# Two-layer graph network: one picked tile fewer per iteration in each layer

## Chip, cores and metric

The kernel runs on one core of a Trainium2 chip. The metric is the device time of one execution in microseconds (us); a lower time is better. The kernel before took 6166.7 us (median of 3 runs, 6165.09 to 6170.27).

## The reference

A graph has 12500 nodes of 32 features and 400000 edges, each with a source node `src` and a destination node `dst`, sorted by `dst`. Two layers run one after the other, each on the layer-normed and rectified features.

```
h = relu(layernorm(x))
# layer 0: a small network per edge, mean over the edges of a destination
m   = relu(concat(h[src], edge_attr_16) @ w1a + b1a) @ w1b + b1b
agg = segment_sum(m, dst) / max(count, 1)
x   = x + relu(concat(h, agg) @ w2a + b2a) @ w2b + b2b
h = relu(layernorm(x))
# layer 1: a sum per destination
x   = x + (1 + eps) * h + segment_sum(relu(h[src] + edge_attr_32), dst)
```

The costly step is `h[src]`: for each of the 400000 edges one row has to be fetched by an index.

## The kernel before, in words

**Tiles, chunks, iterations.** 128 edges make a tile, five tiles a chunk (slot k = 0 to 4), five chunks an iteration. There are 125 iterations of 25 tiles in each layer. All of it is written out by hand, with counting semaphores between the engines; a `Turn` is an iteration, written as half and offset so that two iterations stand in one loop body, and `sum_near_windows(layer, scope)` holds the loops of both layers.

**Two ways to fetch rows.** A tile's 128 source rows come in one of two ways. *Gathered*: GpSimd (POOL) issues an indirect DMA that reads them from DRAM (`gathers`, the issue is recorded at L953), from `projected_rows` (the source part already multiplied by w1a) in layer 0 and `hidden_rows` in layer 1. *Picked*: all nodes lie in SBUF as `part_high` and `part_low`, node = 100 * partition + block, in 7 pieces of 14 blocks (the last of 16). For each piece TensorE multiplies the pieces by a 0/1 matrix `owner_hot`, which selects a partition for each edge (`sum_pieces`, L977): 14 matmuls per picked tile. VectorE then selects the block within the piece with one multiply and one reduction (`select`, L1218 and L1229). In layer 0 the picked rows are transposed on TensorE (`turn_pick`, L991), copied by ScalarE into the lower 32 rows of the chunk's edge block (`copy_pick`, L1091), and enter the chunk's edge product (`edge_products`, L998) as further rows of the contraction, so that bank columns of that tile hold the whole sum. In layer 1 they are written where a gather would have put them.

`PICK_TABLE` lists the picked tiles: slot, tile, row in the owner list, place. Seven exist: tile 4 of each slot, tile 3 of slots 1 and 3. Layer 0 uses the five of tile 4, so 20 tiles per iteration are gathered; layer 1 uses all seven and gathers 18. `tiles_in(k, parity)` is how many tiles of chunk k are gathered, `picks_of(k, turn)` which picks it has.

**Hot rows.** ScalarE makes `owner_hot` for the next iteration in three batches, slots 0 and 1, 2 and 3, and 4 (`make_hots`): seven squares per batch (L1080) and one relu over the batch (L1085). Their size goes with the number of picks in the batch.

**The order within a step.** Each engine runs through k = 0 to 4. TensorE in step k: `sum_pieces` for slot k + 3 (layer 1: k + 2), in layer 0 the edge product of slot k + 1 and the transpose of slot k + 2, then `scatter` of chunk k - 1, a one-hot product that sums messages by destination into a window of 48 nodes (L1007). VectorE: add of the edge part to the gathered rows (`add_edges`, L1251), in layer 1 the split in two parts (L1258, L1262), window add (L1273), one-hot of the destinations (L1233), then `select`. ScalarE: relu (`rectify`, L1103 and L1105 in layer 0, L1098 in layer 1), edge load at k = 0, `copy_pick`, `make_hots`.

**What holds the gathers.** Before the gathers of chunk k POOL waits until the chunk's buffer has been rectified in the iteration before (`rectified`), and for pacing until picks further ahead have been summed (`pieces_summed`) and, halfway through the chunk, until half of the next pick is (`halves_summed`); `picks_ahead` says which. The gathers of the first iteration have no pacing wait. One semaphore per slot counts landed gathers, and `add_edges` waits for it.

**Between the layers** stand the mean, the node network of layer 0, the second layer norm and the split, which the change does not touch, and after each loop a check for edges outside the windows. Its semaphore counts are worked out from `LAYER_PICKS[0]`.

Of the kernel before, what the change touches and what calls it, by code (L numbers as in the profile page):

```python
# [6 lines left out]
P = 128  # L7
# [4 lines left out]
TILES = 5  # L12
CHUNK = TILES * P
SLOTS = 5
# [13 lines left out]
ACT = mybir.ActivationFunctionType  # L28
# [6 lines left out]
PICK_TABLE = (Pick(0, 4, 1, 0), Pick(1, 4, 2, 1), Pick(1, 3, 0, 5), Pick(2, 4, 3, 2), Pick(3, 4, 4, 3),  # L35
              Pick(3, 3, 5, 6), Pick(4, 4, 6, 4))
PICK_ROWS = len(PICK_TABLE)

LAYER_PICKS = ((tuple(pick for pick in PICK_TABLE if pick.tile == TILES - 1),) * 2,
               (PICK_TABLE, PICK_TABLE))  # L40

BATCH_SLOTS = ((0, 1), (2, 3), (4,))
BATCH_OF_SLOT = (0, 0, 1, 1, 2)
# [5 lines left out]
def number(turn):  # L49
    return 2 * turn.half + turn.offset  # L50


def odd(turn):
    return turn.offset % 2
# [6 lines left out]
def before(turn, even_count, odd_count):  # L61

    passed = even_count * ((turn.offset + 1) // 2) + odd_count * (turn.offset // 2)
    return (even_count + odd_count) * turn.half + passed
# [9 lines left out]
def since(homes, n):  # L74


    count = len(homes)
    for back in range(1, count + 1):
        if homes[(n - back) % count] == homes[n]:
            return back  # L80


def gnn_kernel(nc, x, src_cols, src_picks, dst_cols, dst_rows, edge16, edge32, w1a, b1a, w1b_t, b1b,
# [4 lines left out]
    PICK_ROW = P - D  # L88
    CHUNKS = edge16.shape[0]
    H1 = b1a.shape[0]  # L90
# [45 lines left out]
    with ExitStack() as ctx:  # L136
# [3 lines left out]
        def sem(name):  # L140
            return ctx.enter_context(nc.semaphore(name))
# [58 lines left out]
        def edge_t(k, parity):  # L200
            return edges[:, parity * SLOTS + k, 0:P]
        gathered = [sb(f"gathered{k}", [P, TILES, H1]) for k in range(SLOTS)]
        messages = sb("messages", [P, SLOTS * TILES, SUMS])
        message = [messages[:, k * TILES:(k + 1) * TILES, :] for k in range(SLOTS)]
# [4 lines left out]
        bank = [ctx.enter_context(nc.psum_tensor(f"bank{k}", [P, PSUM_COLS], F32)) for k in range(8)]  # L209
# [126 lines left out]
        def piece_of(part, j):  # L336

            b = piece_blocks(j)
            return part[0:NP, b.start * D:b.stop * D].rearrange("p (f b) -> p f b", f=D)
# [47 lines left out]
        def gathered_rows(k, row):  # L387

            flat = gathered[k][:, :, :].rearrange("p t n -> p (t n)")[:, 0:TILES * row]
            return flat.rearrange("p (t n) -> p t n", n=row)  # L390
# [14 lines left out]
        def prepare(scope):  # L405
# [58 lines left out]
            with nc.Block() as block:  # L464
# [165 lines left out]
                def _(dve):  # L630
# [48 lines left out]
                    nc.vector.memset(ln_eps[:, :], LN_EPS).then_inc(ln_eps_ready, 1)  # L679
                    nc.vector.memset(zero_col[:, :], 0.0)  # L680
                    nc.vector.memset(edges[64:PICK_ROW, :, 0:P], 1.0)
                    dve.wait_ge(counted, 2)
                    nc.vector.tensor_copy(window_f[:, :], window_i[:, :])
                    nc.vector.tensor_scalar(minus_piece[:, :], piece_i[:, :], -1.0, None, ALU.mult)
# [37 lines left out]
        def sum_near_windows(layer, scope):  # L722
# [3 lines left out]
            width, row, table = (SUMS, H1, projected_rows) if layer == 0 else (2 * D, D, hidden_rows)  # L726
# [9 lines left out]
            summed = sem(f"summed{layer}")  # L736
            picks = LAYER_PICKS[layer]
            PICKS = [len(some) for some in picks]
            ROUND = sum(PICKS)
# [8 lines left out]
            picks_copied = sem("picks_copied") if layer == 0 else None  # L748
# [60 lines left out]
            def pick_hot(pick, j, parity):  # L809

                b = BATCH_OF_SLOT[pick.slot]
                hots = batch_hot(b, parity).rearrange("p (j s e) -> p j s e", j=PIECES, e=P)
                return hots[:, j, pick.row - rows_of_batch(picks[parity], b).start, :]

            if layer == 0:
                LOOK, SELECT = 3, 3
                edge_home = [k % 3 for k in range(SLOTS)]
                pick_home = [5 + n % 2 for n in range(ROUND)]
                wide_home = [0, 1, 2, 0, 1] * 2
            else:  # L820
                LOOK, SELECT = 2, 1
                pick_home = [0, 1, 2, 5, 6, 7, 0, 1, 2, 5, 6, 7, 2, 5]
            window_banks = (3, 4)

            summands = width if layer == 0 else SUMMANDS
# [17 lines left out]
            def picks_of(k, turn):  # L843
                return [n for n, pick in enumerate(picks[odd(turn)]) if pick.slot == k]

            def tiles_in(k, parity):
                return TILES - sum(pick.slot == k for pick in picks[parity])

            def picks_before(turn):
                return before(turn, *PICKS)  # L850

            def chunks_before(turn):
                return before(turn, SLOTS, SLOTS)

            def place_in_round(n, turn):
                return n + (PICKS[0] if odd(turn) else 0)
# [22 lines left out]
            with nc.Block(no_gpsimd_drain=True) as block:  # L879
# [87 lines left out]
                def _(pe):  # L967
                    def sum_pieces(n, turn, early=False):

                        pick, home = picks[odd(turn)][n], place_in_round(n, turn)  # L970
                        if n == picks_of(BATCH_SLOTS[BATCH_OF_SLOT[pick.slot]][0], turn)[0]:
                            pe.wait_ge(owners_hot[BATCH_OF_SLOT[pick.slot]], number(turn) + 1)
                        if early or layer and since(pick_home, home) < 6:
                            pe.wait_ge(pieces_placed, picks_before(turn) + (n + ROUND + 1 - since(pick_home, home)))
                        for m, (j, part) in enumerate(products_of_a_pick):
                            rows = piece_of(part, j)
                            last = nc.tensor.matmul(  # L977
                                bank[pick_home[home]][:, 0:PITCH * D].rearrange(
                                    "p (f b) -> p f b", b=PITCH)[:, :, 0:rows.shape[2]],
                                pick_hot(pick, j, odd(turn)), rows,  # L980
                                start=(m == 0), stop=(m == len(products_of_a_pick) - 1))
                            if m == len(products_of_a_pick) // 2 - 1:
                                last.then_inc(halves_summed, 1)
                        last.then_inc(pieces_summed, 1)
# [9 lines left out]
                    def edge_products(k, turn):  # L994
                        if k == 0:
                            pe.wait_ge(edge_in, 16 * number(turn) + 16)
                        pe.wait_ge(picks_copied, picks_before(turn) + (picks_of(k, turn)[0] + ROUND + 1))
                        nc.tensor.matmul(bank[edge_home[k]][:, 0:TILES * H1], edge_t(k, odd(turn)),  # L998
                                         w_edge[:, :, :].rearrange("p t n -> p (t n)"),
                                         start=True, stop=True).then_inc(multiplied, 1)  # L1000
# [37 lines left out]
                    for k in range(LOOK):  # L1038
                        for n in picks_of(k, FIRST):
                            sum_pieces(n, FIRST, early=layer == 0 and n >= 2)  # L1040
# [26 lines left out]
                def _(act):  # L1067
# [26 lines left out]
                    def rectify(k, turn):  # L1094

                        if layer:
                            act.wait_ge(rows_split, chunks_before(turn) + (k + 1))
                            nc.scalar.activation(message_parts[:, k, :, 0:2 * D], message[k][:, :, 0:2 * D],  # L1098
                                                 ACT.Relu).then_inc(rectified, 1)
                        else:  # L1100
                            act.wait_ge(added, chunks_before(turn) + (k + SLOTS + 1))
                            tiles = tiles_in(k, odd(turn))
                            nc.scalar.activation(message[k][:, TILES - 1, 0:row],  # L1103
                                                 bank[edge_home[k]][:, (TILES - 1) * H1:TILES * H1], ACT.Relu)
                            nc.scalar.activation(message[k][:, 0:tiles, 0:row], gathered_rows(k, row)[:, 0:tiles, :],  # L1105
                                                 ACT.Relu).then_inc(rectified, 1)

# [257 lines left out]
        def sum_far_windows(layer):  # L1365
# [6 lines left out]
            gather_in = gathers_in[0]  # L1372
            near = [TILES - sum(pick.slot == k for pick in LAYER_PICKS[0][0]) for k in range(SLOTS)]
            gathers_done = [16 * ITERS * (near[k] + TILES * layer) for k in range(SLOTS)]
# [331 lines left out]
        with ExitStack() as own:  # L1706
            self_part = sb("self_part", [P, BLOCKS, H2], scope=own)
            with ExitStack() as scope:
                prepare(scope)
            with ExitStack() as scope:  # L1710
                sum_near_windows(0, scope)
                sum_far_windows(0)
            with ExitStack() as scope:
                update_nodes(scope)
        with ExitStack() as scope:
            sum_far_windows(1)
            sum_near_windows(1, scope)
# [32 lines left out]
```

## Time and profile before

| | |
|---|---|
| median of 3 runs | 6166.7 us |
| profiled execution, its own time | 6167.25 us |
| its span, first to last instruction | 6165.2 us |
| granted TensorE clock, mean | 0.991 |
| layer 0, first to last gather | 63 to 3199 us |
| layer 1, first to last gather | 3291 to 6134 us |
| busy, PE / VectorE / ScalarE / GpSimd | 5919.7 / 3754.2 / 4351.2 / 4544.9 us |

Times are microseconds unless marked ns. PE is the matmul side of TensorE, PEld its weight loads, DVE VectorE, ACT ScalarE, POOL GpSimd. A matmul's shown duration overlaps the next one's, so the pace of PE is read from start times. For POOL, busy is the issue of an indirect DMA; what stands in brackets is idle time just before and what ended it. "issue" there means that the profile shows nothing that it waited for.

### The profile page before, as it was taken

The page shows a single profiled execution, that of the slowest core. Times are in us where ns is not written, and L with a number is a line of the kernel's source. Part 1 is how long each engine was busy: PE and PEld are TensorE (multiplying, and loading weights), DVE is VectorE, ACT ScalarE, POOL GpSimd, SP SyncE. Part 2 cuts the span into 40 slices and gives each one's busy share as a digit, 9 for nine tenths or more (in the row PEclk, how much of TensorE's full clock was granted, in tenths as well). Part 3 has the DMA queues.
Part 4 walks back from the last instruction along what each step waited for, and adds up shares of the span by engine and source line. Part 5 has one row for each costly group of instructions (what it writes and reads, how often), then busy time and mean ns, then how long its engine had stood idle before and what let it go on. Part 6 is the DMA issues. An engine that isn't in the chain of part 4 may idle for free. (4 is left out here: it accounts for less than half of the span.)

```text
span 6165.2 us, 106642 instructions
## 1 busy us (share of the span) xinstructions
PE 5919.7 (96%) x32834; PEld 5085.6 (82%) x32835; DVE 3754.2 (61%) x9052; ACT 4351.2 (71%) x8692; POOL 4544.9 (74%) x4799
## 2 busy tenths in 40 slices
PE   7999999999999999999988999999999999999999
PEld 5887777777777777777777888888888888888888
DVE  6554444444444444444447777777777777777776
ACT  5766666666666666666656777777777777777775
POOL 5777777777777777777755777777777777777776
PEclk9999999999999999999998999999999999999999
DMA  4222222222222222222221222222221222222221
GB/s 116 66 69 65 65 65 67 66 67 65 65 65 68 65 66 65 65 65 68 65 50 45 52 52 51 49 53 53 52 51 48 53 52 52 50 50 52 53 53 41
DMA packets 331462, 367.43 MB, mean 60 GB/s; under 512 B 87161, under 2 KB 256536, under 8 KB 331166
## 3 DMA queue, kind: packets, MB, share of 16 engines
q0 software_dynamic: 152000, 160.05, 13.8%
q1 hardware_dynamic: 46276, 130.67, 6.5%
q10 hardware_dynamic: 133146, 76.25, 4.4%
q8 instruction: 17, 0.28, 0.0%
q14 instruction: 23, 0.19, 0.0%
HBM read 358.17 MB, written 8.46 MB: 59 GB/s over the span
## 5 line engine op out<-in xcount | busy, mean ns | idle before, releaser
L977 PE MATMUL bank<-part_high,owner_hot 125*128 125x448 f32 (+1 forms) x10500 | 4011.6, 382 | 181.3 <-ACT owner_hot L1085 147.9
L977 PE MATMUL bank<-part_low,owner_hot 125*128 125x448 f32 (+1 forms) x10500 | 3897.7, 371 | 0.0
L953 POOL DMA_INDIRECT gathered<-projected_rows,indices x2500 | 2368.5, 947 | 779.2 <-issue 692.6
L953 POOL DMA_INDIRECT gathered<-hidden_rows,indices x2250 | 2151.7, 956 | 693.7 <-issue 576.0
L977 PEld LDWEIGHTS bank<-part_high,owner_hot 125*128 125x128 f32 x10500 | 1980.7, 189 | 414.1 <-ACT owner_hot L1085 162.3
L977 PEld LDWEIGHTS bank<-part_low,owner_hot 125*128 125x128 f32 x10500 | 1979.4, 189 | 197.7 <-issue 0.2
L1080 ACT ACTIVATE owner_hot<-owner_in,minus_piece 125x256 fp32r<-125x256 f32 (+2 forms) x3948 | 1591.6, 484 | 37.9 <-PE bank L977 11.6
L1085 ACT ACTIVATE owner_hot<-owner_hot 125x1792 fp32r<-125x1792 f32 (+1 forms) x750 | 1276.0, 1701 | 23.8
L1218 DVE SCALAR_TENSOR_TENSOR hidden<-window_f,places_now,bank 128x512 f32<-128x512 f32 x1500 | 1101.7, 734 | 121.8 <-PE bank L977 121.4
L1251 DVE TENSOR_TENSOR gathered<-gathered,bank 128x384 f32<-128x384 f32 x625 | 346.0, 554 | 1323.6 <-DMA gathered<-projected_rows,indices 1257.2
L1103 ACT ACTIVATE messages<-bank 128x96 f32<-128x96 f32 x625 | 157.5, 252 | 923.4 <-DVE gathered L1251 917.0
L1098 ACT ACTIVATE message_parts<-messages 128x320 fp32r<-128x320 f32 x625 | 292.6, 468 | 640.1 <-DVE messages L1262 640.1
L1007 PEld LDWEIGHTS bank<-hidden,messages 128*97 128x97 f32 x6250 | 601.8, 166 | 168.7 <-issue 160.0
L1007 PE MATMUL bank<-hidden,messages 128*97 128x48 f32 x6250 | 613.9, 245 | 5.0 <-ACT messages L1105 5.0
L1229 DVE TENSOR_REDUCE gathered<-hidden 128x32 f32<-128x512 f32 x875 | 600.2, 686 | 30.2
L998 PE MATMUL bank<-w_edge,edges 128*128 128x480 f32 x1250 | 607.3, 567 | 4.4 <-ACT edges L1091 4.4
L1080 ACT ACTIVATE owner_hot<-hidden,minus_piece 125x384 fp32r<-125x384 f32 x1302 | 585.6, 531 | 19.3 <-issue 14.6
L1251 DVE TENSOR_TENSOR gathered<-gathered,edges 128x160 f32<-128x160 f32 x625 | 205.7, 329 | 489.0 <-DMA gathered<-hidden_rows,indices 470.2
L1229 DVE TENSOR_REDUCE wide_rows<-hidden 128x32 f32<-128x512 f32 x625 | 428.8, 686 | 21.5
L1007 PEld LDWEIGHTS bank<-onehot_r,message_parts 128*66 128x66 f32 x3125 | 277.3, 139 | 84.1 <-ACT message_parts L1098 35.0
L1105 ACT ACTIVATE messages<-gathered 128x384 f32<-128x384 f32 x625 | 323.4, 517 | 0.0
L1007 PE MATMUL bank<-onehot_r,message_parts 128*66 128x48 f32 x3125 | 270.4, 213 | 15.3 <-ACT message_parts L1098 14.2
(125 smaller groups left out, 2478.1 us busy)
## 6 DMA issues: line engine op xcount, KB each, us to landing
owner_in<-owner_rows SPq DMA_DIRECT2D x188, 448.0 KB
edges<-in_edge ACTq DMA_DIRECT2D x124, 400.0 KB
gathered<-projected_rows,indices POOLq DMA_INDIRECT x2500
gathered<-hidden_rows,indices POOLq DMA_INDIRECT x2250, 2.4
hidden<-owner_rows SPq DMA_DIRECT2D x62, 448.0 KB
edges<-in_edge ACTq DMA_DIRECT2D x124, 200.0 KB
projected_rows<-projected SPq DMA_DIRECT2D x25, 168.0 KB
sources<-in_src_cols SPq DMA_DIRECT2D x1, 1562.5 KB, 6.8
```

Source lines behind the costliest of these rows:

```text
L953: pool.indirect_dma_start(gathered_rows(k, row)[:, t, :], None, table, bass.IndirectOffsetOnAxis(ap=index(k, odd(turn))[:, t:t + 1], axis= ...
L977: last = nc.tensor.matmul(bank[pick_home[home]][:, 0:PITCH * D].rearrange("p (f b) -> p f b", b=PITCH)[:, :, 0:rows.shape[2]], pick_hot(pi ...
L998: nc.tensor.matmul(bank[edge_home[k]][:, 0:TILES * H1], edge_t(k, odd(turn)), w_edge[:, :, :].rearrange("p t n -> p (t n)"), start=True, s ...
L1007: last = nc.tensor.matmul(bank[window_home(k, turn)][0:summands, 0:WINDOW], summand(k, t), onehot[k][:, t, :], start=(t == 0), stop=(t == ...
L1080: last = nc.scalar.activation(hots[:, j, :], rows, ACT.Square, bias=minus_piece[0:NP, j:j + 1], scale=1.0)
L1085: nc.scalar.activation(whole_batch, whole_batch.bitcast(F32), ACT.Relu, bias=1.0, scale=-1.0).then_inc(owners_hot[b], 1)
L1098: nc.scalar.activation(message_parts[:, k, :, 0:2 * D], message[k][:, :, 0:2 * D], ACT.Relu).then_inc(rectified, 1)
L1103: nc.scalar.activation(message[k][:, TILES - 1, 0:row], bank[edge_home[k]][:, (TILES - 1) * H1:TILES * H1], ACT.Relu)
L1105: nc.scalar.activation(message[k][:, 0:tiles, 0:row], gathered_rows(k, row)[:, 0:tiles, :], ACT.Relu).then_inc(rectified, 1)
L1218: nc.vector.scalar_tensor_tensor(out=placed[:, :, :], in0=spread(window_f[:, 0:PITCH], D, 1), scalar=places_now[:, odd(turn), pick.place:p ...
L1229: nc.vector.tensor_reduce(rows, placed[:, :, :], AX.X, ALU.add).then_inc(picked, 1)
L1251: nc.vector.tensor_tensor(rows, rows, other, ALU.add).then_inc(added, 1)
```

## The change

Slot 3 loses one pick in each layer. In layer 0 its tile 4, its only pick, is gathered instead: four picks (slots 0, 1, 2 and 4) and 21 gathers per iteration. In layer 1 its tile 3 is gathered: six picks and 19 gathers. The rest of the diff follows from a chunk without a pick in layer 0: the rows of its edge block that held picked rows are zeroed once at the start; the edge product waits for as many copied picks as the chunk has, here none; the relu of the picked tile from the bank is left out where all five tiles are gathered; the first pick of a batch is looked for over the batch's slots. The lists of buffers that picks rotate through (`wide_home`, `pick_home`) get the new lengths. In layer 1 the new `pick_home` returns to a bank every six picks. The owner list and its load keep all seven rows.

```diff
-LAYER_PICKS = ((tuple(pick for pick in PICK_TABLE if pick.tile == TILES - 1),) * 2,
-               (PICK_TABLE, PICK_TABLE))
+LAYER_PICKS = ((tuple(pick for pick in PICK_TABLE if pick.tile == TILES - 1 and pick.slot != 3),) * 2,
+               (tuple(pick for pick in PICK_TABLE if (pick.slot, pick.tile) != (3, 3)),) * 2)
...
                     nc.vector.memset(edges[64:PICK_ROW, :, 0:P], 1.0)
+                    for slot in range(SLOTS):
+                        if all(pick.slot != slot for pick in LAYER_PICKS[0][0]):
+                            for parity in range(2):
+                                nc.vector.memset(edge_t(slot, parity)[PICK_ROW:P, :], 0.0)
...
-                wide_home = [0, 1, 2, 0, 1] * 2
+                wide_home = [0, 1, 2, 0, 1, 2, 0, 1]
...
-                pick_home = [0, 1, 2, 5, 6, 7, 0, 1, 2, 5, 6, 7, 2, 5]
+                pick_home = [0, 1, 2, 5, 6, 7] * 2
...
-                        if n == picks_of(BATCH_SLOTS[BATCH_OF_SLOT[pick.slot]][0], turn)[0]:
+                        if n == min(m for slot in BATCH_SLOTS[BATCH_OF_SLOT[pick.slot]] for m in picks_of(slot, turn)):
...
-                        pe.wait_ge(picks_copied, picks_before(turn) + (picks_of(k, turn)[0] + ROUND + 1))
+                        for n in picks_of(k, turn):
+                            pe.wait_ge(picks_copied, picks_before(turn) + (n + ROUND + 1))
...
-                            nc.scalar.activation(message[k][:, TILES - 1, 0:row],
-                                                 bank[edge_home[k]][:, (TILES - 1) * H1:TILES * H1], ACT.Relu)
+                            if tiles < TILES:
+                                nc.scalar.activation(message[k][:, TILES - 1, 0:row],
+                                                     bank[edge_home[k]][:, (TILES - 1) * H1:TILES * H1], ACT.Relu)
```

## Rows read from the trace of the kernel before

**Rows 1.** The page: busy time by engine, and shares of the chain that ended last.
```profile
PE 5919.7 (96%) x32834; PEld 5085.6 (82%) x32835; DVE 3754.2 (61%) x9052; ACT 4351.2 (71%) x8692; POOL 4544.9 (74%) x4799
...
PE 33%; DVE 4%; ACT 3%; DMA 2%; issue 2%; DVEq 2%; POOL 1%; ACTq 0%; POOLq 0%; PEldq 0%
```

**Rows 2.** Waits over the whole span: total us, times, longest us.
```profile
POOL gathered L953 <- PE bank L977: 160.9, 528, 0.3
```

**Rows 3.** Timeline of POOL, layer 0: start, duration, instruction, [idle before].
```profile
2005.69 0.94 POOL L953 DMA_INDIRECT gathered<-projected_rows,indices  x1 [0.31 <-PE bank L977]
```

**Rows 4.** Stretches: length; busy of PE, PEld, DVE, ACT, POOL (instructions); PE clock; DMA share; GB/s.
```profile
125.00:3199.00 3074.00, 2945.88 (x16642) 2448.28 (x16641) 1494.89 (x3449) 2084.09 (x4801) 2324.13 (x2462) 1.00 0.28 66
...
3345.00:6134.00 2789.00, 2746.17 (x15128) 2437.54 (x15127) 2073.24 (x5165) 2112.25 (x3553) 2114.72 (x2214) 1.00 0.21 51
```

**Rows 5.** Instructions by group, 1000 to 2500 us: count, busy us, mean ns, idle before.
```profile
L953 POOL DMA_INDIRECT gathered<-projected_rows,indices x1202 | 1134.9, 944 | 366.3 <-issue 337.3 <-PE bank L977 28.9
```

**Rows 6.** The same, 4000 to 5500 us.
```profile
L953 POOL DMA_INDIRECT gathered<-hidden_rows,indices x1191 | 1138.1, 956 | 362.9 <-issue 300.4 <-PE bank L977 52.4 <-ACT message_parts L1098 10.1
```

**Rows 7.** Timeline of PE, layer 0, one step and the iteration's one wait.
```profile
2002.45 0.48 PE L977 MATMUL bank<-part_high,owner_hot 125*128 125x512 f32 x1
...
2005.48 0.97 PE L998 MATMUL bank<-w_edge,edges 128*128 128x480 f32 x2
...
2007.19 0.48 PE L977 MATMUL bank<-part_high,owner_hot 125*128 125x512 f32 x1
...
2013.12 0.50 PE L977 MATMUL bank<-part_high,owner_hot 125*128 125x512 f32 x1 [1.00 <-ACT owner_hot L1085]
```

**Rows 8.** Timeline of PE, layer 1, a step with one pick.
```profile
5002.66 0.48 PE L977 MATMUL bank<-part_high,owner_hot 125*128 125x512 f32 x1
...
5005.92 0.48 PE L977 MATMUL bank<-part_high,owner_hot 125*128 125x512 f32 x1
```

**Rows 9.** Timeline of DVE at the start of the kernel.
```profile
1.26 1.12 DVE L681 MEMSET edges<- 32x1280 f32 x1 [0.30 <-issue]
2.92 0.59 DVE L683 CAST window_f<-window_i 128x48 f32<-128x48 int32 x1 [0.53 <-POOL piece_i L569]
```

**Rows 10.** Timeline of POOL at the start of layer 0.
```profile
79.32 3.39 POOL L953 DMA_INDIRECT gathered<-projected_rows,indices  x1 [0.30 <-issue]
...
93.79 0.94 POOL L953 DMA_INDIRECT gathered<-projected_rows,indices  x1 [3.58 <-ACT messages L1105]
...
101.16 0.95 POOL L953 DMA_INDIRECT gathered<-projected_rows,indices  x1 [2.69 <-ACT messages L1105]
...
106.79 0.94 POOL L953 DMA_INDIRECT gathered<-projected_rows,indices  x1 [0.94 <-ACT messages L1105]
```

**Rows 11.** Timeline of ACT, layer 0: hots of two rows and of one.
```profile
100.66 2.90 ACT L1080 ACTIVATE owner_hot<-owner_in,minus_piece 125x256 fp32r<-125x256 f32 x7
103.59 1.70 ACT L1085 ACTIVATE owner_hot<-owner_hot 125x1792 fp32r<-125x1792 f32 x1
...
110.42 2.16 ACT L1080 ACTIVATE owner_hot<-owner_in,minus_piece 125x128 fp32r<-125x128 f32 x7
112.61 0.95 ACT L1085 ACTIVATE owner_hot<-owner_hot 125x896 fp32r<-125x896 f32 x1
```

**Rows 12.** Timeline of POOL at the start of layer 1.
```profile
3321.00 0.94 POOL L953 DMA_INDIRECT gathered<-hidden_rows,indices  x1 [5.58 <-issue]
...
3330.42 0.94 POOL L953 DMA_INDIRECT gathered<-hidden_rows,indices  x1 [0.98 <-issue]
...
3339.86 0.94 POOL L953 DMA_INDIRECT gathered<-hidden_rows,indices  x1 [0.90 <-issue]
```

**Rows 13.** Timeline of PE at the start of layer 1.
```profile
3296.63 0.80 PE L977 MATMUL bank<-part_high,owner_hot 125*128 125x512 f32 x1 [15.77 <-ACT owner_hot L1085]
...
3302.13 0.49 PE L977 MATMUL bank<-part_high,owner_hot 125*128 125x512 f32 x1
...
3320.05 0.43 PE L1007 MATMUL bank<-onehot_r,message_parts 128*66 128x48 f32 x5
```

## The prediction, made before the result was known

> **What bounds the kernel now.** I read the page first, then the waits, then GpSimd's own rows. The page [rows 1] invites a wrong answer: PE is busy 96% of the span and leads the chain of waits with 33%, GpSimd (POOL) shows 74%. The chain's shares add up to 47% of the span, about what layer 1 and the end take, and where engines run side by side it stays on the one it is on.
>
> So I asked who waits. In the whole span POOL waits for PE 528 times, never longer than 0.3 us [rows 2]. 0.30 us is the gap between any two gathers, put down to PE [rows 3] or to nothing. It is there too in the first round of gathers [rows 10], which has no pacing wait in the code. So it belongs to the instruction. One gather costs POOL 0.94 + 0.30 = 1.248 us, and POOL never pauses: in layer 0 from 125 to 3199 us it starts 2462 gathers in 3074 us, 1.2486 us each; in layer 1 from 3345 to 6134 us 2214 in 2789 us, 1.2597 us each [rows 4]. Its 74% is the 0.94 out of 1.248. In layer 1 the mean busy time is 956 ns against 944 [rows 5, 6], the reason for its 12 ns more.
>
> A steady iteration is therefore gathers times this interval: layer 0 has 20 (25 tiles less 5 picks), 25.0 us; layer 1 has 18, 22.7 us.
>
> PE's own need is close but below. In layer 0 a step (pick, edge product, transpose, scatter) takes 2007.19 - 2002.45 = 4.74 us, of which the pick is 3.03 and the rest 1.71 [rows 7]. Five steps make 23.7 us of 25.0, and the remainder shows as one wait of 1.00 us for the hot rows. In layer 1 a step with one pick takes 5005.92 - 5002.66 = 3.26 us, 2.99 of it the pick [rows 8]: 7 x 2.99 + 5 x 0.27 = 22.3 us of 22.7. The two engines are nearly balanced; POOL is the longer one in both layers.
>
> **The change part by part.**
>
> *Picks removed.* One per iteration and layer. PE loses 14 matmuls and, in layer 0, a transpose: 3.0 us per iteration. ACT loses a third to a half of one batch of hot rows and, in layer 0, two small copies; DVE loses one multiply and one reduction, about 1.4 us. None of this is on POOL, so in the steady loop it is worth nothing: PE's need falls to 20.7 of 26.2 us and to 19.3 of about 23.9 us, and what is late next is still POOL.
>
> *Gathers added.* One per iteration and layer: 21 and 19. Each goes into POOL's stream behind no cover. Bounds for one: 1.248 us (layer 0's interval) and 1.260 us (layer 1's). I take 1.248 for both. The extra in layer 1 comes in single gathers, and I count it as belonging to VectorE's work per chunk, which stays. 125 x 1.248 = 156.0 us per layer, 312.0 us in all.
>
> *Pacing waits.* Gathers of a chunk wait for picks of the same iteration. With four picks the middle of chunk 4's gathers in layer 0 now waits for half of chunk 4's own pick, formerly chunk 3's. PE does that pick in step 1, behind the scatter of chunk 4 of the iteration before. POOL gets there 19 gathers (23.7 us) after that chunk's last gather, and scatter and half a pick need some 10 us. It costs nothing; were the cover gone, POOL would stand by the difference, and everything behind it. In layer 1 the one pick fewer brings the release forward.
>
> *Edge product of chunk 3, layer 0.* It no longer waits for a copied pick. All five tiles come from bank columns added by VectorE; the add grows from 4 to 5 tiles, beside POOL's work. Its extra relu goes away. Nothing on the path.
>
> *Two memsets on VectorE at the start*, each a tenth of the 32 x 1280 one that takes 1.12 us [rows 9]. They stand ahead of a wait of 0.53 us for POOL's ramps, and are covered there; uncovered at most 0.3 us. I take 0.
>
> *Start of layer 0.* Here POOL does wait: gaps of 3.58, 2.69 and 0.94 us instead of 0.30 [rows 10]. The first ends when ACT has rectified chunk 0, which hangs on offsets, picks 0 to 2 and ACT's order, none of them changed. So the first iteration's extra gather is done in that wait: minus 1.25 us. The second hangs on chunk 1 behind the next iteration's first hots, also unchanged. The third ends with chunk 2's rectify, behind ACT's hots for chunks 2 and 3; with one row instead of two the final step falls from 1.70 to 0.95 us [rows 11] and the seven squares by 0.74 us, so the 0.64 us over the usual gap goes. Layer 0: 156.0 - 1.25 - 0.64 = 154.1 us. Bounds: 156.0 with nothing absorbed, 149.7 if all three waits (7.21 - 0.90 = 6.3 us) went.
>
> *Start of layer 1.* Gaps of 5.58, 0.98 and 0.90 us [rows 12]. The first waits until PE has summed all seven picks of iteration 0: it starts at 3296.63 and has the seventh done when the scatter at 3320.05 begins [rows 13]. One pick fewer brings that forward by 2.9 us, to about 3318.1 for POOL, while POOL arrives one gather later; so of 5.28 us above the usual gap some 1.1 us stay. The second (0.68 above) hangs on three picks that are all still made and stays. The third hung on chunk 3's two picks and goes. Saved: 4.2 + 0.6 = 4.8 us. Layer 1: 156.0 - 4.8 = 151.2 us. Bounds: 156.0 and 149.4; with 1.260 us per gather 1.5 us more.
>
> *Between the layers and at the end* nothing changes: the last chunk's gathers, landing, add and scatter are chunk 4's.
>
> **Sum.** 154.1 + 151.2 = 305.3 us on the profiled execution's 6167.25 us (span 6165.2 and 2 us around it) gives 6472.6 us. The median of the runs, 6166.7, is 0.5 us lower, so I say 6472 us, 5.0% slower. Single long gathers (3.39 us [rows 10] beside 0.94) can land anywhere and move a run by a few us.
>
> **Rivals.**
>
> *PE is the bound of layer 1, as the chain says.* Then the extra gather there is free and each iteration shrinks by the pick, 3.0 us, down to POOL's 19 x 0.944 = 17.9 at best: 19.3 instead of 22.7 us, -425 us, with +154 in layer 0: about 5900 us, faster. For it: the 33%, PE's 98% busy in the stretch [rows 4]. Against: POOL's gap would have to stretch at times when it waits, and after 3339.86 us it never does. It decides if PE's need is above 18 x 1.26 = 22.7 us; I count 22.3. Chance 1%; that the same held in layer 0 too lies within it.
>
> *The clock.* PE's idle time in layer 0 grows from 1.3 to 5.5 us per iteration, much of it in the step that has no pick. Where the engine had stood idle (15.77 us) before 3296.63, its matmuls ran at 1.2 GHz and a pick took 3302.13 - 3296.63 = 5.50 us [rows 13] instead of 3.03. One pick per iteration at that clock costs 2.5 us, inside the 5.5 us spare. An iteration wholly at that clock needs 4 x 5.50 + 5 x 3.42 = 39.1 us; past about 30% of the work at the low clock PE passes POOL's 26.2 us. Half of it: 29.9 us, 125 x 3.7 = 460 us more, some 6930 us. Against: work without a break brought the clock back within that first pick, so a loop that falls behind heals itself. Chance 3%. The Trainium skill (TensorE: Matmul & The Clock Gate, section "HAM oscillation — how this bites in real kernels") says that a loop in which TensorE waits for data in each round can come back at the low clock every round; by that rule alone the full 39.1 us, 7930 us in all, would be the ceiling, which no row here shows.
>
> *Gathers get dearer.* 21 of them leave the same spacing but more traffic; if layer 0's became like layer 1's, 0.012 x 2625 = 31 us more, 6504 us. For it: layer 1 shows it with 5 us less per iteration for the rest. Against: there the traffic per us is lower than in layer 0 (51 against 66 GB/s [rows 4]), so traffic isn't the reason. Chance 6%.
>
> *The extra gather is partly hidden* (more than the starts give back), by picks that free VectorE and shorten gathers in layer 1 to 0.944: 0.012 x 2375 = 28 us less, 6444 us. Chance 6%.
>
> **How the numbers follow.** Forecast 84%, rivals 1, 3, 6 and 6%. The forecast's own spread is 6467 to 6480 (all start waits gone or none), a few us wider for long gathers and between runs. Reaching partly to the two last rivals: 6456 to 6492. Faster by over 0.2% 0.01, within 0.2% (12 us, what a measurement of this kernel can tell) 0.01, slower 0.98.
>
> **What would show it.** POOL's gaps still 0.30 us in both loops; 1000 to 2500 us with the same 1200 gathers or so, iterations of 26.2 and 23.9 us; 2625 and 2375 gathers; layer 1's first wait near 1.4 us instead of 5.6; longer waits of PE for ACT or DVE, with perhaps a clock below 1.00 in layer 0, at no cost. Wrong: POOL gaps above 0.31 us in the loops, or gathers of another mean.

## The result and the profile after

The changed kernel takes 6480.3 us (median of 4 runs, 6479.31 to 6481.2), the one before 6166.75 us (4 runs): ratio 1.0508, interval 1.0489 to 1.0526. The forecast was 6472 us, range 6456 to 6492.

The kernel before took 7439 us when e8 and e9 ran, 6176 us on the same chip later (e10 to e12), and 6166 us beside the other experiments, so e8 and e9 are told apart from the rest.

The page of the changed kernel, engines, TensorE's clock in 40 slices, the chain's shares by engine, and GpSimd's two groups of gathers (busy, mean ns | idle before):

```profile
PE 5592.8 (86%) x29209; PEld 4715.6 (73%) x29210; DVE 3429.0 (53%) x8554; ACT 3930.0 (61%) x8442; POOL 4787.7 (74%) x5049
...
PEclk8999999999999999999988999999999999999998
...
PE 19%; ACT 12%; DMA 4%; issue 4%; DVE 3%; POOL 2%; DVEq 2%; ACTq 1%; POOLq 0%; PEldq 0%
...
L957 POOL DMA_INDIRECT gathered<-projected_rows,indices x2625 | 2484.9, 947 | 818.1 <-issue 793.0
L957 POOL DMA_INDIRECT gathered<-hidden_rows,indices x2375 | 2278.1, 959 | 725.6 <-issue 634.6
```

PE lost ten points of its share [rows 1], and the kernel became 313 us longer. (PE's busy time fell by only 327 us, though 250 picks at 3.0 us are about 750 us of work by my estimate: part of what is left now runs at a lower clock.) POOL's share is 74% as before: its stream is as dense as it was, only longer. The stretches of the two loops (busy of PE, PEld, DVE, ACT, POOL, then PE clock, DMA share, GB/s), and the group in the same 1500 us as [rows 5]:

```profile
3520.00:6446.00 2926.00, 2546.30 (x13277) 2235.90 (x13275) 1887.93 (x4877) 1923.66 (x3522) 2219.87 (x2318) 0.93 0.22 49
130.00:3353.00 3223.00, 2805.34 (x14791) 2268.93 (x14792) 1341.24 (x3198) 1840.53 (x4549) 2436.30 (x2582) 0.92 0.28 65
```

```profile
L957 POOL DMA_INDIRECT gathered<-projected_rows,indices x1202 | 1134.3, 944 | 366.3 <-issue 365.1 <-PE bank L981 1.2
```

3223 us over 2582 gathers is 1.2483 us each in layer 0, against 1.2486 [rows 4]; the count in the 1500 us window is the same 1202. 2926 over 2318 is 1.2623 us in layer 1, against 1.2597. From first to last gather layer 0 went from 3136.2 to 3291.6 us (+155.4), layer 1 from 2843.5 to 3001.7 us (+158.2). What lies between and behind moved by 0.1 us, and the first gather starts 0.4 us earlier.

The clock fell from 1.00 to 0.92 and 0.93 [rows 4]. The timeline of PE in layer 0 shows when: it now waits 2.8 us once per iteration, and some of these waits are followed by matmuls at 1.2 GHz.

```profile
2003.55 0.50 PE L981 MATMUL bank<-part_high,owner_hot 125*128 125x512 f32 x1 [2.76 <-ACT owner_hot L1090]
...
2008.11 0.97 PE L1003 MATMUL bank<-w_edge,edges 128*128 128x480 f32 x2
...
2029.79 0.80 PE L981 MATMUL bank<-part_high,owner_hot 125*128 125x512 f32 x1 [2.77 <-ACT owner_hot L1090]
...
2035.28 0.97 PE L1003 MATMUL bank<-w_edge,edges 128*128 128x480 f32 x2
```

Both stretches run from the start of a pick to the edge product behind it. The first pick takes 4.56 us, partly at the low clock; the second, after the same wait, 5.49 us, wholly at the low clock (compare [rows 13] with the 3.03 us of [rows 7]). POOL's gaps stay at 0.30 us through both.

### The profile page after: what moved, and what is told of

Its sections match the earlier page's. It is cut to its first block and busy times, and to the rows that moved or that the text cites. A ratio compares the mean times of both kernels' runs of the same rounds, so it can differ in the third digit from the quotient of the medians.

```text
span 6478.3 us, 98953 instructions
## 1 busy us (share of the span) xinstructions
PE 5592.8 (86%) x29209; PEld 4715.6 (73%) x29210; DVE 3429.0 (53%) x8554; ACT 3930.0 (61%) x8442; POOL 4787.7 (74%) x5049
## 5 line engine op out<-in xcount | busy, mean ns | idle before, releaser
L981 PE MATMUL bank<-part_high,owner_hot 125*128 125x448 f32 (+1 forms) x8750 | 3563.1, 407 | 366.7 <-ACT owner_hot L1090 362.3
L981 PE MATMUL bank<-part_low,owner_hot 125*128 125x448 f32 (+1 forms) x8750 | 3455.4, 395 | 0.0
L957 POOL DMA_INDIRECT gathered<-projected_rows,indices x2625 | 2484.9, 947 | 818.1 <-issue 793.0
L957 POOL DMA_INDIRECT gathered<-hidden_rows,indices x2375 | 2278.1, 959 | 725.6 <-issue 634.6
L981 PEld LDWEIGHTS bank<-part_high,owner_hot 125*128 125x128 f32 x8750 | 1793.1, 205 | 572.7 <-ACT owner_hot L1090 378.6
L981 PEld LDWEIGHTS bank<-part_low,owner_hot 125*128 125x128 f32 x8750 | 1793.3, 205 | 190.0
L1085 ACT ACTIVATE owner_hot<-owner_in,minus_piece 125x128 fp32r<-125x128 f32 (+2 forms) x3948 | 1447.8, 448 | 34.3 <-issue 13.5
L1090 ACT ACTIVATE owner_hot<-owner_hot 125x1792 fp32r<-125x1792 f32 (+1 forms) x750 | 1087.3, 1450 | 23.8
L1224 DVE SCALAR_TENSOR_TENSOR hidden<-window_f,places_now,bank 128x512 f32<-128x512 f32 x1250 | 919.0, 735 | 110.2 <-PE bank L981 107.6
L1235 DVE TENSOR_REDUCE gathered<-hidden 128x32 f32<-128x512 f32 x750 | 514.5, 686 | 25.9
```

Source lines behind the costliest of these rows:

```text
L957: pool.indirect_dma_start(gathered_rows(k, row)[:, t, :], None, table, bass.IndirectOffsetOnAxis(ap=index(k, odd(turn))[:, t:t + 1], axis= ...
L981: last = nc.tensor.matmul(bank[pick_home[home]][:, 0:PITCH * D].rearrange("p (f b) -> p f b", b=PITCH)[:, :, 0:rows.shape[2]], pick_hot(pi ...
L1085: last = nc.scalar.activation(hots[:, j, :], rows, ACT.Square, bias=minus_piece[0:NP, j:j + 1], scale=1.0)
L1090: nc.scalar.activation(whole_batch, whole_batch.bitcast(F32), ACT.Relu, bias=1.0, scale=-1.0).then_inc(owners_hot[b], 1)
L1224: nc.vector.scalar_tensor_tensor(out=placed[:, :, :], in0=spread(window_f[:, 0:PITCH], D, 1), scalar=places_now[:, odd(turn), pick.place:p ...
L1235: nc.vector.tensor_reduce(rows, placed[:, :, :], AX.X, ALU.add).then_inc(picked, 1)
```

## The experiments

The theory: GpSimd's stream of indirect DMAs sets both loops. Rivals: the lower clock costs the time; TensorE sets the loops. The two halves of the change, picks away and gathers added, were done one without the other (e1, e2), then one gather was taken away from the kernel before (e3), then each layer was changed alone (e5, e6). The rest looks at the part the sum missed, and at the pacing waits. A and B below are these two rivals. Diffs are shortened where "..." stands.

**e1_picks_off.** The changed kernel without the added gathers.

```diff
+            def tiles_fetched(k, parity):
+                return tiles_in(k, parity) + (GATHERS_MORE if k == 3 else 0)   # GATHERS_MORE = -1
...
-                        for t in range(tiles_in(k, odd(turn))):
+                        for t in range(tiles_fetched(k, odd(turn))):
```

> The changed kernel, but the tile of slot 3 that is no longer picked isn't gathered either (the edges of that tile are left out of the result): 20 and 18 gathers per iteration with 4 and 6 picks. Theory (GpSimd's stream of gathers sets both loops): 6161 us, 6155 to 6167, about 5 us under the kernel before by the shorter start waits, though the mean TensorE clock falls to 0.92 to 0.95. Rival A (the added 313 us come from TensorE's lower clock, 0.923 in the changed kernel against 0.991): about 6480 us, for the picks are gone here too. Rival B (TensorE sets the loops): 125 x 3.0 us less per layer where it is the bound, 5790 us for one layer, 5420 for both.

Measured: 6165.1 us, ratio 1.000 (0.999 to 1.0009), clock 0.939, with GpSimd's stream as in the kernel before:

```profile
L962 POOL DMA_INDIRECT gathered<-projected_rows,indices x2500 | 2367.5, 947 | 781.1 <-issue 754.2
L962 POOL DMA_INDIRECT gathered<-hidden_rows,indices x2250 | 2154.5, 958 | 689.6 <-issue 575.5
```

The picks gone, and nothing gained: 3 us of TensorE's work per iteration, 14 matmuls, were free in both layers. The lower clock alone costs nothing, which ends rival A; TensorE sets neither loop, which ends rival B.

**e2_gather_on.** The kernel before, all picks kept, with the added gathers.

```diff
+GATHERS_MORE = 1
...
                             rows = gathered_rows(pick.slot, row)[:, pick.tile, :]
+                            if (pick.slot, pick.tile) == (3, 3):
+                                rows = wide_rows[0][:, 0:row]
```

> The kernel before with all its picks, and the same tile of slot 3 gathered as well (in layer 0 it is added on top, in layer 1 the pick goes to a spare tile, so the result counts or drops that tile's rows wrongly): 21 and 19 gathers with 5 and 7 picks. Theory: 6476 us, 6470 to 6485, with the clock near 0.99 and GpSimd's gap still 0.30 us. Rival A (clock): 6167 us. Rival C (the missing picks let gathers run better or worse in the changed kernel): differs from the changed kernel's 6480 us by more than 10 us.

Measured: 6479.7 us, ratio 1.0511 (1.0495 to 1.0527), clock 0.973. The changed kernel's time, with TensorE's full work:

```profile
L957 POOL DMA_INDIRECT gathered<-projected_rows,indices x2625 | 2486.1, 947 | 818.1 <-issue 750.9
L957 POOL DMA_INDIRECT gathered<-hidden_rows,indices x2375 | 2275.1, 958 | 729.6 <-issue 609.1
```

The 250 gathers bring the whole 313 us. Rival C of the expectation falls too: the two kernels differ by 0.6 us. Whether a gather's 1.248 us are GpSimd's own work or are set by the queue that takes its orders, no run separates.

**e3_gather_off.** The kernel before, picks kept, one gather fewer per iteration and layer (that tile is left out of the result): `GATHERS_MORE = -1`, and the unfetched buffer zeroed once.

> The kernel before with all its picks and one gather fewer per iteration and layer, in slot 3 (stale rows stand in for that tile): 19 and 17 gathers. Theory: TensorE's need that I read as 23.7 and 22.3 us now meets GpSimd's 23.7 and 21.4 us: layer 0 gains 1.0 to 1.25 us per iteration, layer 1 0.3 to 0.4 us, 5965 to 6005 us, and GpSimd's gap grows in layer 1. Rival (GpSimd alone sets the loops down to there): 6167 - 312 = 5855 us. Rival B (TensorE sets them): 6167 us, unchanged.

Measured: 5948.6 us, ratio 0.965 (0.9635 to 0.9664). This is lower than I said (5965 to 6005), and far above 5855. The windows show where the gain stops:

```profile
1000.00:2400.00 1400.00, 1400.00 (x7974) 1168.87 (x7973) 716.91 (x1653) 999.22 (x2302) 1058.39 (x1122) 1.00 0.27 67
4000.00:5400.00 1400.00, 1400.00 (x7778) 1259.38 (x7776) 1075.91 (x2655) 1092.87 (x1831) 1025.88 (x1075) 1.00 0.21 52
```

and in layer 1 POOL's timeline has what the kernel before has nowhere in its steady loop, a longer gap once per iteration:

```profile
5002.02 0.94 POOL L958 DMA_INDIRECT gathered<-hidden_rows,indices  x1 [1.02 <-issue]
...
5024.15 0.94 POOL L958 DMA_INDIRECT gathered<-hidden_rows,indices  x1 [0.95 <-issue]
```

PE is 100% busy in both. In layer 0 POOL still runs 1400 / 1122 = 1.248 us per gather, 19 of them 23.7 us, the number I read as PE's need: the engines meet there. The longer gap of layer 1 says "issue", yet 122 times it stands before the first gather of chunk 4, where the code waits for six summed picks and for the rectified chunk: "issue" is no proof that nothing was waited for. In layer 1 an iteration is 5024.15 - 5002.02 = 22.1 us, PE's need, a little under my 22.3; 17 gathers would take 21.4. From first to last gather layer 0 takes 2983.5 us (-152.7) and layer 1 2777.1 us (-66.3), 22.2 us per iteration: in the steady loop layer 0 got the whole 1.25 us where I had allowed for less (3.3 us of it went back in a longer first wait, 6.87 us instead of 3.58), and layer 1's need was read 0.1 to 0.2 us too high.

**e5_layer0_only, e6_layer1_only.** `LAYER_PICKS` and the buffer list of the other layer as before.

> The change in layer 0 alone; layer 1 keeps its seven picks. Theory: one gather interval per iteration, less what the start hides: +155 us, 6321 us (6316 to 6327), layer 0 from first to last gather 3292 us, layer 1 unchanged at 2843 us. Rival (the layers act on each other, as by the owner list, the clock or the scratch in between): layer 1's stretch differs by more than 5 us.

> The change in layer 1 alone. My sum of before gave 151 us, the changed kernel showed 158 us, of which 8.5 us is more time in long gathers (0.97 to 1.5 us). Theory: that belongs to the changed order of layer 1 and comes back here: +158 us, 6325 us (6320 to 6330), long gathers 33 us over 0.944 in sum. Rival (it differs from execution to execution): +151 us, 6318 us, long gathers near 24.5 us.

Measured: 6318.5 us (1.0249, 1.0232 to 1.0266) and 6317.4 us (1.0246, 1.0228 to 1.0263). In e5 layer 0 takes 3291.1 us and layer 1 2840.8, as expected. In e6 layer 1 takes 2993.4 us, +149.9, where the changed kernel had +158.2. So the two alone come to 152.1 + 151.1 = 303.2 us, and both together to 313.6. These 10 us are no more than the intervals of the ratios allow, so the times alone don't show that the layers act on each other; the traces show where the difference lies. My theory for e6 fell: the 8 us don't come with layer 1's own change. The rival (it differs from execution to execution) has the time right, 6317.4 us and 24.4 us in long gathers, but the three traces of kernels with both changes (the changed kernel, e10, e11) all have 31 to 33 us there. The difference is in the mean of layer 1's gathers, e6 first, the changed kernel run again (e10) second:

```profile
L957 POOL DMA_INDIRECT gathered<-hidden_rows,indices x2375 | 2269.5, 956 | 725.9 <-issue 634.7
```

```profile
L957 POOL DMA_INDIRECT gathered<-hidden_rows,indices x2375 | 2281.6, 961 | 725.9 <-issue 641.6
```

Idle time is the same to 0.3 us (725.6 in the changed kernel); busy time is 8.6 us (2278.1 - 2269.5) to 12.1 us more for the same 2375 gathers. e10 had all gathers 2 ns longer, also in layer 0.

**e4_mask_by_tensor_tensor, e7_mask_later, e12_no_mask_again** look at the long gathers of layer 1: of 2250 some 340 take 0.97 to 1.1 us, 24.5 us over 0.944 in sum; layer 0 has one, of 1.11 us. In the timelines two thirds of them are gathers in which VectorE starts its mask (L1258) 0.125 to 0.375 us into the gather: from 4000 to 4800 us all 39 with an offset from 0.25 on, 21 of 36 from 0.125 to 0.25, and none of the 101 outside. The other third, 113 in the whole layer, have no mask there but the one-hot of the destinations (L1233), nearly all 0.125 to 0.25 us in. The edits, in short form:

```diff
 e4: nc.vector.tensor_scalar(high, rows, 12, 12, shift right, shift left)
  -> nc.vector.tensor_tensor(high, rows, high_mask, ALU.bitwise_and)
 e7: + nc.vector.tensor_tensor(spare[:, 0, :], spare[:, 1, :], spare[:, 1, :], ALU.add)   # ahead of the mask
 e12: the mask left out, the subtraction follows the add
```

> The kernel before, computing the same: VectorE's mask of the high bits in layer 1 (the TENSOR_SCALAR with two shifts) is done as a TENSOR_TENSOR and with a constant tile. Gathers in layer 1 take 956 ns on average against 944 in layer 0, and long ones (1.03 us) lie over this instruction. Theory: that instruction holds the gathers up; without it their mean falls to 944 to 948 ns, and the time to 6142 us, 6138 to 6152. Rival (traffic, the copies per iteration or another instruction does it): mean stays 956 ns, 6167 us.

> The kernel before with a needless VectorE addition of 128x160 (0.33 us) between the add and the mask of layer 1; computes the same. In the kernel before long gathers are those in which the mask starts 0.125 to 0.375 us after the gather's start, and the type of the mask's instruction made no difference. Theory M (the mask's start in that phase makes the gather long): they are again those with the mask at 0.125 to 0.375 us. Theory A (the add before it, or the landing that releases it, does): they are now those with the mask at about 0.49 to 0.74 us. Time 6167 us, 6160 to 6175, in either case.

> The kernel before without layer 1's mask instruction (its sums are wrong), again. Theory (the mask's own accesses lengthen gathers): 6143 us, long gathers gone. Rival (another instruction in that place does it as well): 6166 us (6160 to 6170), the long gathers remain, with the subtraction in the mask's place.

Measured: e4 6166.1 us (1.0001, 0.9992 to 1.001), gathers 956 ns; e7 6167.1 us in its one execution; e12 6175.6 us where the kernel before took 6176.4 (0.9997, 0.9988 to 1.0007). Three variants, three times no change, and the long gathers in each. In e12 they have the subtraction in the mask's place:

```profile
5000.03 0.99 POOL L953 DMA_INDIRECT gathered<-hidden_rows,indices  x1 [0.31 <-issue]
5000.24 0.33 DVE L1258 TENSOR_TENSOR messages<-gathered,messages 128x160 f32<-128x160 f32 x1
...
5003.83 0.95 POOL L953 DMA_INDIRECT gathered<-hidden_rows,indices  x1 [0.31 <-issue]
5003.85 0.34 DVE L1251 TENSOR_TENSOR gathered<-gathered,edges 128x160 f32<-128x160 f32 x1
5004.22 0.33 DVE L1258 TENSOR_TENSOR messages<-gathered,messages 128x160 f32<-128x160 f32 x1
```

In e7 long were those with the mask 0.25 to 0.5 us in (34 of 46 up to 0.375, then 22 of 22, then 0 of 44). Theory A's 0.49 to 0.74 us took the mask to move by some 0.36 us behind the add (L1253). It moved by 0.12: the kernel before has 0.36 us from the start of the add to that of the mask, e7 with its spare addition has 0.48.

```profile
5001.38 0.32 DVE L1253 TENSOR_TENSOR gathered<-gathered,edges 128x160 f32<-128x160 f32 x1 [1.14 <-DMA gathered<-hidden_rows,indices]
5001.62 0.32 DVE L1259 TENSOR_TENSOR spare<-spare 128x160 f32<-128x160 f32 x1
5001.85 0.31 DVE L1261 TENSOR_SCALAR messages<-gathered 128x160 int32<-128x160 int32 x1
```

So counted from the mask the window moved by as much as the mask did, and counted from the add it stayed, which is theory A's answer. Theory M would have it at 0.125 to 0.375 us again. Counted by the add over all of layer 1, a gather is long whenever the add starts 0.05 to 0.15 us before it: 186 of 186 in the kernel before, 181 of 181 in e4, 154 of 154 in e7, 194 of 194 in e12. Where the add starts more than 0.2 us before the gather or after its start, it is long in one case of e7 and in none of the others. The mask is not the cause. Whether the add is, or the landing that releases it, or something later in VectorE's chain, is open, and so are the third of the long gathers that go with the one-hot.

**e10_changed_again, e11_no_pacing_again.** The pair that tests the pacing waits: e11 is the changed kernel with both removed.

```diff
-                            pool.wait_ge(pieces_summed, picks_before(turn) + (ROUND + picks_ahead(k, turn)))
...
-                                pool.wait_ge(halves_summed, picks_before(turn) + (picks_ahead(k, turn) + 1))
```

> The changed kernel once more, as the partner of the next two, since the runs without pacing and without mask met a chip on which the kernel before took 7439 us instead of 6166. Theory: 6480 us (6476 to 6484) where the kernel before takes 6166 us, layer 1's long gathers again near 33 us over 0.944 (a property of the kernel), or near 24.5 us (a property of the execution). On the other kind of chip: the gathers aren't the only bound, and the ratio of 1.051 isn't kept.

> The changed kernel without GpSimd's waits for summed picks, again. Theory as before: 6480 us (6474 to 6484), gap 0.30 us. Rival (the pacing itself keeps something from being held up, as the 1.20 of the last run suggests): well over 6500 us, with GpSimd waiting for ScalarE and idle times of TensorE put down to nothing.

Measured, on one chip with the kernel before at 6176.4 us: 6490.9 us (1.0507, 1.049 to 1.0525) and 6490.1 us (1.0506, 1.0489 to 1.0524). Both lie above the times that I had named, by the 10 us by which everything was longer there; the ratio is the changed kernel's. The long gathers of layer 1 in e10 have 31.4 us over 0.944, near the 33 that I had named for a property of the kernel. Waits of POOL without pacing:

```profile
POOL gathered L955 <- issue: 1499.6, 4918, 0.3
POOL gathered L955 <- ACT message_parts L1101: 22.3, 73, 0.3
```

No gap got shorter, and no entry "<- PE" is left. So the 0.30 us belong to the gather. The 528 entries "<- PE" of [rows 2], never longer than 0.3 us, then name a signal that fell into this gap; e11 shows it for the changed kernel, for the kernel before it is inferred.

**e8_no_mask, e9_no_pacing.** The same edits, first try.

> The kernel before without the mask instruction of layer 1 (stale high parts stand in, so layer 1's sums are wrong); the subtraction follows the add directly. Long gathers of layer 1 (24.5 us over 0.944 in sum) came with the mask's start 0.125 to 0.375 us into the gather. Theory (the mask's own reads and writes lengthen the gather): they go, 6143 us, 6140 to 6150. Rival (anything in that place of the chain, or the landing before it): they stay with the subtraction in that place, 6166 us, 6160 to 6170.

> The changed kernel without GpSimd's waits for summed picks; only the wait for the rectified chunk and for the indices stands. Theory (the waits have long been met, the 0.30 us gap belongs to the gather): gaps stay 0.30 us, 6480 us, 6474 to 6483. Rival (part of the gap is these waits and their two extra instructions, so that the gather stream is longer than need be): gaps fall below 0.30 us at the chunk starts and halves, 10 places per iteration and layer, 6480 - 2500 x 0.05 = 6355 us for 0.05 us each.

Measured against a kernel before of 7439 us: 7436.9 us (0.9997, 0.9987 to 1.0006) and 8925.9 us (1.1997, 1.1947 to 1.2047). e8 shows that the mask is worth nothing there either. Here POOL's stream was not the only bound: in e8 its gap is above 0.35 us 664 times, in the kernel before at 6167 us 8 times. In e9 it waits for ScalarE, and TensorE idles with nothing named:

```profile
POOL gathered L955 <- ACT message_parts L1101: 1274.7, 178, 11.3
POOL gathered L955 <- ACT messages L1109: 1188.1, 217, 13.3
PE bank L979 <- issue: 1185.6, 963, 8.4
```

The changed kernel with its pacing was not run under that condition, so how much of the 20% is the missing pacing is not known. e10 and e11 answer the question only where the kernel before takes 6166 to 6176 us.

## Why the prediction was right, and where it was off

*POOL bounds both loops.* Right: e1 and e2 separate it cleanly, and the interval per gather is the same to 0.0003 us in layer 0. The one sign that I had named against it and that came is "gathers of another mean", in layer 1 (below).

*Removed picks are worth nothing.* Right (e1, 1.000).

*250 gathers at 1.248 us, 312.0 us.* Right for layer 0, +155.4 us with the start (forecast 154.1). In layer 1 it was too low (below).

*Start of layer 0.* The mechanism held, the size of the first wait didn't:

```profile
95.65 0.94 POOL L957 DMA_INDIRECT gathered<-projected_rows,indices  x1 [4.63 <-ACT messages L1111]
...
103.40 0.94 POOL L957 DMA_INDIRECT gathered<-projected_rows,indices  x1 [3.07 <-ACT messages L1111]
```

2.3 us was forecast, 4.63 came. But with layer 0 as before the wait was 5.77 us in e4, 5.66 in e6, 5.89 in e7 and 5.77 in e12; [rows 10] with 3.58 was the short one. One execution is a poor witness for such a wait. The number of gathers per iteration shows in it: 6.87 us with 19 (e3), 5.66 to 5.89 with 20 (5.12 in e8, at the slow time), 4.63 with 21 (e5 4.66, e11 4.63; e2 4.28). So the extra gather is absorbed there, about 1.2 us. The two short ones, 3.58 and 2.17 in e10, belong to the two executions in which the long gather near 80 us is the 14th and not the 15th. The third wait went, as forecast, and in e1, e5 and e11; in e2, which keeps two rows in that batch of hots, it is still 0.94 us, but e10 has 1.24 us.

*Start of layer 1.* 5.58 became nothing above 0.42 us; I had left 1.1 and 0.7 us over the gap.

```profile
3451.64 0.80 PE L981 MATMUL bank<-part_high,owner_hot 125*128 125x512 f32 x1 [16.26 <-ACT owner_hot L1090]
...
3456.28 0.40 PE L981 MATMUL bank<-part_high,owner_hot 125*128 125x512 f32 x1
```

```profile
3445.57 4.23 POOL L957 DMA_INDIRECT gathered<-hidden_rows,indices  x1 [1.96 <-ACTq L1140]
...
3481.57 0.94 POOL L957 DMA_INDIRECT gathered<-hidden_rows,indices  x1 [0.42 <-issue]
```

In the changed kernel the first pick took 4.64 us instead of 5.50, since the clock came back earlier, and POOL arrived later, with one gather of 4.23 us where the kernel before had one of 3.45. In e6 one gap of 0.82 us is left. Layer 1 in e6, +149.9 us, meets my 151.2.

*The term that was mis-sized* is layer 1's gather at 1.248 us in the changed kernel. Layer 1 took 158.2 us more and not 151.2. Its mean gather rose from 956 to 959 ns, 2.9 ns x 2375 = 7 us; a further 1.5 us is that the added gathers cost layer 1's mean and not layer 0's, and the start gave 1.3 us of it back. I had named the long gathers as VectorE's per chunk and unchanged. They are tied to a place in the chunk, but not unchanged. A gather costs about 0.12 us more where the mask starts 0.25 to 0.375 us into it, and on average 0.05 us more from 0.125 to 0.25. In the changed kernel 206 and 141 chunks of layer 1 lie in these two places (31.7 us), in e6 118 and 226 (23.7 us), in e10 193 and in e11 202 in the first. The price of a place is the same; with layer 0 changed too more chunks lie in the dear one. Why VectorE's work falls there is not shown.

*Single long gathers.* I wrote that they can land anywhere. Those of 3 us and more don't: see the last section.

*The clock.* It fell to 0.92, as named, at no cost. Of the 121 picks of layer 0 that follow a wait of 2.0 to 2.8 us for hot rows, 33 took 5.4 to 5.5 us, 73 took 4.2 to 5.1 us, and 15 took 3.0 us. The Trainium skill (TensorE: Matmul & The Clock Gate, section "HAM oscillation — how this bites in real kernels") describes a loop in which TensorE's wait brings the low clock back in every round. This trace agrees only in part, since 15 rounds of the 121 show no low clock. The cost stayed inside TensorE's 5.5 us to spare: e2 has 0.973 and the same time. The 7930 us of that rival was added up wrongly: it leaves out the extra gather of layer 1. On the base of 6472 us, 125 x (39.1 - 26.2) gives about 8085 us; nothing near either was seen.

## What to carry to other kernels

Look for the engine whose gap between instructions never changes, not for the one with the highest busy share or the longest chain: here 74% busy with a constant 0.30 us gap was full, 96% busy had slack. Such a gap can carry the name of another engine or none; removing the wait in the code (e11) tells whether it is one. Test the reading with two half-changes, the relief alone and the load alone; here they gave 1.000 and 1.051. When two engines are balanced to 2 to 5%, moving work to the fuller one costs its whole price and the relief of the other returns nothing; e3 shows how far relief of the fuller one goes before the other takes over. No split of the tiles by whole picks per iteration that was run beats the kernel before; only splits with fewer picks were run.

## What the runs showed of the hardware

- An indirect DMA of 128 rows takes GpSimd 0.944 + 0.30 us in layer 0, whether or not the pacing waits stand ahead of it (e11). With rows of 128 bytes in layer 1 instead of 384 it is the same, except for the long gathers.
- A gather of layer 1 takes 0.12 us more when VectorE's add starts 0.05 to 0.10 us before it (84 of 84 in the kernel before, 155 of 155 in the changed one), and nothing more when the add starts after it. Which of the two engines' work meets there is open.
- Two gathers near the start of layer 0, at about 80 and 117 us, and one of the first four of layer 1 take 3.3 to 6.6 us instead of 0.94, in 13 of the 14 traces (the first of them in [rows 10]); e9 lacks the one at 117 us.
- TensorE waits of 2.8 us are followed by the low clock in most iterations and not in others, in the same kernel and at the same place (15 of 121 picks in layer 0 took 3.0 us, 33 took 5.4 to 5.5 us).
- The same program took 7439 us on a chip at one time, 20% longer than the 6176 us at another; removing the pacing waits is free at the second and was not tried against its partner at the first.
